# Gain and shift of three normalizations in a transformer block: two fused VectorE passes in place of one VectorE and two GpSimd passes

## The chip, the core and the metric

One NeuronCore of a Trainium2 chip runs the whole kernel. The metric is device time in microseconds, median of several executions. The kernel before ran in 1309.01 us (median of three, 1305.8 to 1310.01).

## What is computed

The input x has 16 batches of 512 nodes with 128 features. Four graph layers follow one another, each fed with relu(layernorm(x)) and added to x. The last layer is a Chebyshev step with a transformer block, and three of its normalizations have a learned gain and shift:

```python
def _layernorm(x, g, b):
    mu = x.mean(-1, keepdims=True)
    var = ((x - mu) ** 2).mean(-1, keepdims=True)
    return (x - mu) / jnp.sqrt(var + EPS_LN) * g + b
...
h = xp @ Wc + bc
h = _layernorm(h, g1, be1)
h = jax.nn.relu(h)
x1 = h + x
...
```

The attention output with x1 as residual goes through the second normalization (g2, be2), then a feed-forward part with gelu (W1, b1, W2, b2), and its result plus residual through the third (g3, be3). g and be are rows of 128 features, the same for every node; mean and variance are one number per node.

## The kernel before

**Layout.** Nodes lie on the 128 partitions in four groups (`NT` = 4), features along the free dimension. A batch of one tensor is thus a tile of 128 x 4 x 128 float32. The rows g1, be1, g2, be2, g3, be3 lie in `rowv`, repeated on every partition; `row[name]` is a 128 x 128 view, `row4(name)` (line 109) the same broadcast over the four groups.

**Stages.** After a front part (constants, the first layer) the function `build_layers` (line 1524) runs a software pipeline over the 16 batches with five stages: gat, edge, cheb, att, ffn (line 1268). In one iteration each stage works on another batch. Every stage is a list of named steps, and each engine executes its own written-out order of them: `FILL_ORDER` for the first iterations, `ORDER` for the loop, `DRAIN_ORDER` for the last ones (lines 1311 to 1519). `run` (line 1643) goes through these lists. Engines execute their steps strictly in that order and meet each other only through semaphores (`ready` and `freed`).

**A normalization** with tag n1, n2 or n3, on y1, y2 or y3, is this sequence: `ln_stats` (four bn_stats, one for each group, VectorE), `ln_aggr` (four bn_aggr giving mean and variance in `mv`, VectorE), `ln_rstd` (GpSimd: add epsilon, then a power of minus one half, into `rs`; lines 1605 and 1607), `ln_apply` (VectorE, line 1632, four tensor_scalar: subtract the mean, times the reciprocal deviation), `affine_g` (GpSimd, line 1637: times the gain row, one instruction over 128 x 512) and `affine_b` (GpSimd, line 1641: plus the shift row). After n1 stands `cheb_x1` (VectorE, line 1911: relu and residual), after n2 `ffn_turn` (TensorE, line 2136: four transposes of y2), after n3 `ffn_final` (VectorE, line 1974).

**The order around n2 and n1 in the loop.** VectorE: `att_scale att_mask2 att_mask3 ffn_y2 n2_stats n2_aggr gat_apply n2_apply att_mask4 cheb_y n1_stats n1_aggr att_mask5 n1_apply gat_scores0 gat_scores1 att_mask6 gat_scores2 att_mask7 gat_scores3 cheb_x1 ... ffn_y3 att_mask8`; and later `n3_stats edge_rden edge_attn edge_u n3_aggr att_mask13 cheb_klow att_mask14 n3_apply att_mask15`. ScalarE: `gat_wh_out0 gat_wh_out1 att_copy2 ffn_x2T att_exp5 att_copy3 ffn_gelu0 ffn_gelu1 att_exp6`. TensorE: `cheb_g gat_turn att_turn2 att_score5 gat_wh ffn_turn att_turn3 gat_s2 ffn_up0 att_score6 ffn_up1 att_turn4 att_score7 ffn_down0 ffn_down1 cheb_x1turn att_turn5 att_score8`. GpSimd: `cheb_rstd edge_rstd ffn_res gat_rstd edge_lo n2_rstd n2_g n2_b n1_rstd n1_g n1_b ffn_b2 gat_low0 ... gat_low3 n3_rstd n3_g n3_b`. `ffn_b2` (line 1740) adds the b2 row to y2 once `ffn_turn` has read it.

**Attention.** For each of 16 tiles TensorE computes a score tile (`att_score`, line 2005), VectorE adds the mask and takes a minimum (`att_mask`, line 1924), ScalarE takes the exponential (`att_exp`, line 1779), TensorE transposes (`att_turn`, line 2106) and ScalarE copies back (`att_copy`, line 1787). `ffn_x2T` is at line 1759, the gelus at line 1769, `ffn_down0` and `ffn_down1` at line 2148. The transposes of `gat_turn` are at line 299, `gat_apply` at line 243.

Of the kernel before, what the change touches and what calls it, by code (L numbers as in the profile page):

```python
# [11 lines left out]
ALU = mybir.AluOpType  # L12
# [5 lines left out]
NT = N // P  # L18
# [325 lines left out]
def build_front(nc, k):  # L344
# [3 lines left out]
    with ExitStack() as c:  # L348
# [938 lines left out]
    "cheb": """  # L1287
        cheb_prop0 cheb_prop1 cheb_g cheb_x1turn cheb_q cheb_k cheb_v cheb_stats cheb_aggr cheb_lo cheb_y
        n1_stats n1_aggr n1_apply cheb_x1 cheb_qlow cheb_klow cheb_apply cheb_hi cheb_xpT cheb_x1T cheb_qsplit
        cheb_ksplit cheb_vout cheb_rstd n1_rstd n1_g n1_b cheb_res stack0 stack2 stack1 stack3 store_v  # L1290
    """.split(),
    "att": """
        att_turn14 att_score0 att_score1 att_turn15 att_rows att_pv0 att_pv1 att_score2 att_turn0 att_score3
# [8 lines left out]
    """.split(),  # L1302
    "ffn": """
        ffn_wo ffn_turn ffn_up0 ffn_up1 ffn_down0 ffn_down1 att_scale ffn_y2 n2_stats n2_aggr n2_apply ffn_y3
        n3_stats n3_aggr n3_apply ffn_final ffn_x2T ffn_gelu0 ffn_gelu1 ffn_res n2_rstd n2_g n2_b ffn_b2 n3_rstd
        n3_g n3_b load_ffn store_out
    """.split(),
}
STAGE_OF = {step: stage for stage, steps in STAGE_STEPS.items() for step in steps}
# [25 lines left out]
        att_exp15 att_copy13 att_copy14 cheb_vout att_copy15  # L1335
    """.split(),
    "POOL": """
        cheb_rstd edge_rstd ffn_res gat_rstd edge_lo n2_rstd n2_g n2_b n1_rstd n1_g n1_b ffn_b2 gat_low0 gat_low1
        gat_low2 gat_low3 n3_rstd n3_g n3_b
    """.split(),  # L1340
    "SP": """
        load_x load_ffn stack1+ stack3+ store_v+ edge_store+ cheb_res load_v stack0 stack2 store_out
# [87 lines left out]
    """.split(),  # L1430
    "POOL": """
        edge_rstd:0 gat_rstd:1 edge_lo:0 gat_low0:1 gat_low1:1 gat_low2:1 gat_low3:1 cheb_rstd:0 edge_rstd:1
        gat_rstd:2 edge_lo:1 n1_rstd:0 n1_g:0 n1_b:0 gat_low0:2 gat_low1:2 gat_low2:2 gat_low3:2 cheb_rstd:1
        edge_rstd:2 gat_rstd:3 edge_lo:2 n1_rstd:1 n1_g:1 n1_b:1 gat_low0:3 gat_low1:3 ffn_res:0 gat_low2:3 gat_low3:3
        cheb_rstd:2 edge_rstd:3 gat_rstd:4 n2_rstd:0 n2_g:0 n2_b:0 edge_lo:3 n1_rstd:2 ffn_b2:0 gat_low0:4 n1_g:2
        n1_b:2 gat_low1:4 gat_low2:4 gat_low3:4 n3_rstd:0 n3_g:0 n3_b:0 cheb_rstd:3 ffn_res:1 edge_rstd:4 gat_rstd:5
        n2_rstd:1 n2_g:1 n2_b:1 edge_lo:4 ffn_b2:1 n1_rstd:3 gat_low0:5 gat_low1:5 n1_g:3 n1_b:3 gat_low2:5 gat_low3:5
        n3_rstd:1 n3_g:1 n3_b:1
    """.split(),
    "SP": """  # L1440
        load_x:1 load_x:2 edge_store:0 cheb_res:0 stack0:0 stack2:0 load_x:3 stack1:0 stack3:0 store_v:0 edge_store:1
# [67 lines left out]
        cheb_rstd:14 ffn_res:12 edge_rstd:15 n2_rstd:12 n2_g:12 n2_b:12 edge_lo:15 n1_rstd:14 n1_g:14 ffn_b2:12
        n1_b:14 n3_rstd:12 n3_g:12 n3_b:12 cheb_rstd:15 ffn_res:13 n2_rstd:13 n2_g:13 n2_b:13 n1_rstd:15 n1_g:15  # L1510
        n1_b:15 ffn_b2:13 n3_rstd:13 n3_g:13 n3_b:13 ffn_res:14 n2_rstd:14 n2_g:14 n2_b:14 ffn_b2:14 n3_rstd:14
        n3_g:14 n3_b:14 ffn_res:15 n2_rstd:15 n2_g:15 n2_b:15 ffn_b2:15 n3_rstd:15 n3_g:15 n3_b:15
# [9 lines left out]


def build_layers(nc, k):
    bank, sem, W, row4 = k.bank, k.kept_sem, k.W, k.row4
    with ExitStack() as c:  # L1526
        def sb(name, shape, dt=F32):
            return c.enter_context(nc.sbuf_tensor(name, shape, dt))
# [21 lines left out]
        h3, y1, x1 = (tile("cheb_" + n) for n in ["hs", "y1", "x1s"])  # L1550
# [11 lines left out]
        xrE, y2, y3, x3E = (tile("ffn_" + n) for n in ["xr", "y2s", "y3s", "x3"])  # L1562
# [81 lines left out]

# [81 lines left out]
        @block.gpsimd  # L1726
        def _(pool):
            def ffn_res(n):
                ready(pool, "ffn_xr", n, 16, 16)
                nc.gpsimd.tensor_tensor(xrE[:], xrE[:], row4("bo"), ALU.add).then_inc(sem("ffn_res"), 1)  # L1730

            def edge_lo(n):
                ready(pool, "edge_hhi", n)
                freed(pool, "edge_gathered", n)
                nc.gpsimd.tensor_tensor(h2_lo[:], h2[:], h2_hi[:].bitcast(F32), ALU.subtract
                                        ).then_inc(sem("edge_hlo"), 1)

# [79 lines left out]
        def _(dve):  # L1817
# [81 lines left out]
                ln_stats(dve, "n1", n, y1)  # L1899

            def n1_aggr(n):
                ln_aggr(dve, "n1", n, ("n1_normed", n, NT))

            def n1_apply(n):
                ln_apply(dve, "n1", n, y1, y1)

            def cheb_x1(n):
                ready(dve, "n1_aff", n, 2, 2)
                freed(dve, "x1_turned", n)
                freed(dve, "res_stored", n, 16)  # L1910
                nc.vector.scalar_tensor_tensor(flat(x1), flat(y1), 0.0, flat(h3), ALU.max, ALU.add
                                               ).then_inc(sem("cheb_x1"), 1)
# [79 lines left out]
        def _(pe):  # L1992
# [198 lines left out]
```

## Time and profile before

| what | value |
|---|---|
| median of three executions | 1309.01 us |
| profiled execution, its own time | 1312.6 us |
| its span | 1310.8 us |
| TensorE matmul busy | 1159.2 us, 88% |
| VectorE busy | 791.7 us, 60% |
| ScalarE busy | 764.0 us, 58% |
| GpSimd busy | 465.6 us, 36% |
| 33 waits of n_rs on n_mv, GpSimd | 181.1 us |

Busy time is the time in which an engine executes a counted instruction, and its share is of the whole span. The front part lasts until about 450 us, the pipeline fills until about 600, repeats a steady period until about 1150, and drains until 1310.8. A wait is the idle time ahead of an instruction, put down to the event that came last. In timelines PE is TensorE, DVE VectorE, ACT ScalarE and POOL GpSimd. Consecutive VectorE instructions overlap a little in the record, so a group's length is a bit more than the distance to the next start.

### The profile page before, as it was taken

Reading aid. Unit: us, or ns where it says so; the run is one execution under the profiler, and the core shown is the slowest. Engines: PE = TensorE matmul, PEld = TensorE weight load, DVE = VectorE, ACT = ScalarE, POOL = GpSimd, SP = SyncE. Lnnn points to the kernel's source line nnn. Section 1 sums busy time; section 2 is a strip of 40 time slices with the busy share of each in tenths; the row PEclk is TensorE's granted clock in tenths of the full one; section 3 lists DMA queues with packets and bytes.
Section 4 is the critical chain, followed back from the end, with each engine's and each line's share of the span. In section 5 each row is a group of like instructions: output and inputs, shape, how many; then the busy total and the mean of one; then the engine's idle time right before and its main releaser. Section 6 shows DMA issues by size and latency. Waiting matters only on the chain. (4 is left out here: it accounts for less than half of the span.)

```text
span 1310.8 us, 24758 instructions
## 1 busy us (share of the span) xinstructions
PE 1159.2 (88%) x7517; PEld 905.1 (69%) x7517; DVE 791.7 (60%) x2832; ACT 764.0 (58%) x1628; POOL 465.6 (36%) x577
## 2 busy tenths in 40 slices
PE   4989999999996957899998999999999999999763
PEld 3658879888884945676776777777777677666542
DVE  6633213212323525688788888888888888877642
ACT  4213324334211313488788788788888878877770
POOL 4203005003123213235445545634634554543423
PEclk7989999999988978699999999999999999999995
DMA  4001020020200000232423423332432342333320
GB/s 118 13 20 42 25 72 1 26 73 1 65 9 1 17 24 17 63 100 74 113 55 93 113 64 88 104 90 64 118 88 64 104 112 56 96 97 94 100 65 17
DMA packets 123748, 83.68 MB, mean 64 GB/s; under 512 B 13216, under 2 KB 106784, under 8 KB 123680
## 3 DMA queue, kind: packets, MB, share of 16 engines
q1 hardware_dynamic: 123680, 82.82, 23.4%
q8 instruction: 37, 0.61, 0.2%
q14 instruction: 31, 0.25, 0.1%
HBM read 28.25 MB, written 20.97 MB: 38 GB/s over the span
## 5 line engine op out<-in xcount | busy, mean ns | idle before, releaser
L1779 ACT ACTIVATE att_Es<-att_Ts,att_small 128x512 f32<-128x512 f32 x256 | 184.9, 722 | 36.0 <-DVE att_small L1924 33.7
L1924 DVE CUSTOM_DVE_ANT_0 att_Ts<-bank,mask_att 128x512 f32<-128x512 f32 x256 | 173.7, 683 | 49.9 <-PE bank L2005 49.3
L2106 PE MATMUL bank<-ident,att_Es 128*128 128x128 f32 x1024 | 156.0, 275 | 22.2 <-ACT att_PTs L1787 21.2
L1787 ACT COPY att_PTs<-bank 128x512 f32<-128x512 f32 x256 | 148.5, 580 | 37.2 <-PE bank L2106 35.2
L2106 PEld LDWEIGHTS bank<-ident,att_Es 128*128 128x128 f32 x1024 | 119.4, 141 | 63.4 <-issue 29.5
L2005 PE MATMUL bank<-K_parts,Q_parts 128*128 128x512 f32 x256 | 123.3, 492 | 0.0
L502 POOL TENSOR_SCALAR l_rs<-l_mv 128x4 f32<-128x4 f32 x16 | 6.9, 432 | 242.5 <-DVE l_mv L712 242.3
L726 DVE TENSOR_TENSOR P_row<-bank,l_bias 128x512 f32<-128x512 f32 x32 | 22.1, 691 | 115.4 <-PE bank L1119 94.1
L1605 POOL TENSOR_SCALAR n_rs<-n_mv 128x4 f32<-128x4 f32 x48 | 12.2, 255 | 182.5 <-DVE n_mv L1600 181.1
L1109 PE MATMUL bank<-G,x0T 128*128 128x128 f32 x384 | 76.0, 280 | 1.1 <-DVE U2T L721 1.0
L1109 PE MATMUL bank<-G,U1T 128*128 128x128 f32 x384 | 75.1, 278 | 0.0
L1109 PE MATMUL bank<-G,U2T 128*128 128x128 f32 x384 | 75.0, 277 | 0.0
L192 POOL TENSOR_SCALAR gat_Vs<-gat_Ts,gat_small 128x512 f32<-128x512 f32 x64 | 50.6, 807 | 67.1 <-DVE gat_small L268 67.0
L1109 PEld LDWEIGHTS bank<-G,x0T 128*128 128x128 f32 x384 | 61.4, 194 | 5.4 <-issue 2.8
L332 PE MATMUL bank<-gat_whs,gat_ETs 128*128 128x128 f32 x512 | 61.9, 275 | 0.0
L332 PEld LDWEIGHTS bank<-gat_whs,gat_ETs 128*128 128x128 f32 x512 | 60.2, 192 | 0.4 <-ACT gat_ETs L218 0.2
L1109 PEld LDWEIGHTS bank<-G,U1T 128*128 128x128 f32 x384 | 59.3, 195 | 0.0
L1109 PEld LDWEIGHTS bank<-G,U2T 128*128 128x128 f32 x384 | 59.1, 194 | 0.0
L2127 PE MATMUL bank<-att_PTs,v_in 128*32 128x512 f32 x512 | 58.5, 597 | 0.0
L2005 PEld LDWEIGHTS bank<-K_parts,Q_parts 128*128 128x128 f32 x256 | 47.4, 190 | 16.1 <-issue 15.7
L1119 PE MATMUL bank<-Z_hi,P3T_hi 128*128 128x512 f32 x128 | 53.0, 414 | 0.0
L212 ACT ACTIVATE gat_Ts<-gat_Vs,gat_small 128x512 f32<-128x512 f32 x64 | 46.4, 730 | 9.4 <-DVE gat_Vs L272 9.4
(301 smaller groups left out, 3028.0 us busy)
## 6 DMA issues: line engine op xcount, KB each, us to landing
Q_parts<-q_hi SPq DMA_DIRECT2D x128, 64.0 KB, 2.0
Q_parts<-q_lo SPq DMA_DIRECT2D x128, 64.0 KB, 2.0
K_parts<-k_hi SPq DMA_DIRECT2D x128, 64.0 KB, 2.0
K_parts<-k_lo SPq DMA_DIRECT2D x128, 64.0 KB, 2.0
l_x<-in_x SPq DMA_DIRECT2D x16, 256.0 KB, 3.0
P2T<-in_x SPq DMA_DIRECT2D x16, 256.0 KB, 4.6
x_after_l<-P2T SPq DMA_DIRECT2D x16, 256.0 KB, 2.3
gat_xin<-x_after_l SPq DMA_DIRECT2D x16, 256.0 KB, 3.1
```

What stands on the lines that cost most here:

```text
L192: nc.gpsimd.tensor_scalar(g.V[:, t, :], g.T[:, t, :], 0.2, small[:, 5, t:t + 1], ALU.mult, ALU.add).then_inc(sem("gat_low"), 1)
L212: nc.scalar.activation(g.T[:, t, :], g.V[:, t, :], ACT.Exp, bias=small[:, 4, t:t + 1], accum_out=small[:, 6, t:t + 1]).then_inc(sem("gat_e ...
L332: mm = nc.tensor.matmul(a0[:, cols(t)], g.ET[:, s, cols(t)], WhA[:, s, 0:D], start=(s == 0), stop=(s == NT - 1))
L726: nc.vector.tensor_tensor(by_batch(zs[:, t, :]), by_batch(bank[t][:]), bias[:, BLOCKS - 1 - lev, t:t + 1, :].broadcast_to([P, CB, D]), ALU.add
L1109: mm = nc.tensor.matmul(bank[t][:, b * D:(b + 1) * D], UT[i][:, b, cols(t)], G[:, STEPS - k0 - i, :], start=(b == 0 and i == 0), stop=(lev ...
L1119: mm = nc.tensor.matmul(bank[t][:], left[:, s, cols(t)], right[:, s, :], start=False, stop=(s == NT - 1 and i == 2))
L1779: nc.scalar.activation(att_E[:, j % RING_E, :], att_T[:, j % RING_T, :], ACT.Exp, scale=-1.0, bias=att_small[:, 0, j:j + 1], accum_out=att ...
L1787: nc.scalar.copy(att_PT[:, i // NT, :, cols(i % NT)], c2[:].rearrange("p (s q) -> p s q", q=P)).then_inc(sem("att_pt"), 1)
L1924: nc.vector.tensor_tensor_reduce(att_T[:, j % RING_T, :], [c0, c1][j % 2][:], k.mask_att[:, j % NT, :], -QK_SCALE, HUGE, ALU.add, ALU.min, ...
L2005: return nc.tensor.matmul(dst, left, right, start=True, stop=True)
L2106: mm = nc.tensor.transpose(c2[:, cols(s)], att_E[:, i % RING_E, cols(s)], k.ident[:])
L2127: mm = nc.tensor.matmul(b0[r, :], vD[:, s, r], att_PT[:, h, s, :], start=(s == 0), stop=(s == NT - 1))
```

## The change

The two GpSimd passes are gone, and so are their steps `n1_g`, `n1_b`, `n2_g`, `n2_b`, `n3_g`, `n3_b` in all three orders. The gain is now applied before the reciprocal deviation: `ln_gain` computes (x - mean) * g in four VectorE instructions, `ln_shift` computes x * rstd + b in four more. `ln_gain` is called at the end of the steps `n1_aggr`, `n2_aggr`, `n3_aggr`, directly behind the aggregates; `ln_shift` replaces `ln_apply` in `n1_apply`, `n2_apply`, `n3_apply`. The two orders of the operations are the same expression. The consumers wait for four `_aff` events in place of two. VectorE's order of steps is unchanged.

```diff
     "POOL": """
-        cheb_rstd edge_rstd ffn_res gat_rstd edge_lo n2_rstd n2_g n2_b n1_rstd n1_g n1_b ffn_b2 gat_low0 gat_low1
-        gat_low2 gat_low3 n3_rstd n3_g n3_b
+        cheb_rstd edge_rstd ffn_res gat_rstd edge_lo n2_rstd n1_rstd ffn_b2 gat_low0 gat_low1
+        gat_low2 gat_low3 n3_rstd 
...
-        def affine_g(pool, tag, n, x, g):
-            ready(pool, tag + "_normed", n, NT, NT)
-            nc.gpsimd.tensor_tensor(x[:], x[:], row4(g), ALU.mult).then_inc(sem(tag + "_aff"), 1)
-
-        def affine_b(pool, tag, n, x, b):
-            ready(pool, tag + "_aff", n, 1, 2)
-            nc.gpsimd.tensor_tensor(x[:], x[:], row4(b), ALU.add).then_inc(sem(tag + "_aff"), 1)
+        def ln_gain(dve, tag, n, x, g):
+            mv = ln_mem[tag][1]
+            ready(dve, tag + "_aggr", n, NT, NT)
+            for t in range(NT):
+                nc.vector.scalar_tensor_tensor(x[:, t, :], x[:, t, :], mv[:, t, 0:1], row[g], ALU.subtract,
+                                               ALU.mult).then_inc(sem(tag + "_gain"), 1)
+
+        def ln_shift(dve, tag, n, x, b):
+            rs = ln_mem[tag][2]
+            ready(dve, tag + "_gain", n, NT, NT)
+            ready(dve, tag + "_rs", n)
+            for t in range(NT):
+                nc.vector.scalar_tensor_tensor(x[:, t, :], x[:, t, :], rs[:, 1, t:t + 1], row[b], ALU.mult,
+                                               ALU.add).then_inc(sem(tag + "_aff"), 1)
...
             def n1_aggr(n):
-                ln_aggr(dve, "n1", n, ("n1_normed", n, NT))
+                ln_aggr(dve, "n1", n, ("n1_aff", n, NT))
+                ln_gain(dve, "n1", n, y1, "g1")
 
             def n1_apply(n):
-                ln_apply(dve, "n1", n, y1, y1)
+                ln_shift(dve, "n1", n, y1, "be1")
 
             def cheb_x1(n):
-                ready(dve, "n1_aff", n, 2, 2)
+                ready(dve, "n1_aff", n, NT, NT)
...
```

n2 and n3 are changed in the same way as n1.

## Rows read from the trace of the kernel before

**Rows 1.** Busy time in one steady period: window, length, us busy (x instructions) by engine, clock, DMA.
```profile
...
899.93:946.90 46.97, 44.54 (x325) 33.91 (x322) 39.76 (x152) 39.59 (x90) 23.52 (x29) 1.00 0.33 89
...
```

**Rows 2.** TensorE's waits from 600 to 1150: us in total, times, longest.
```profile
...
PE bank L2148 <- ACT ffn_mT L1769: 10.3, 12, 0.9
PE bank L1995 <- POOL ffn_y2s L1641: 9.5, 11, 0.9
...
```

**Rows 3.** VectorE's waits, same stretch.
```profile
...
DVE att_Ts L1924 <- PE bank L2005: 25.6, 39, 1.2
DVE cheb_y L1632 <- POOL n_rs L1607: 9.1, 10, 0.9
...
DVE ffn_y2s L1632 <- POOL n_rs L1607: 7.0, 11, 0.7
...
```

**Rows 4.** VectorE, timeline: start us, us, what, idle before and releaser.
```profile
...
933.37 0.38 DVE L1600 BATCH_NORM_AGGREGATE n_mv<-n_stat 128x2 f32<-128x6 f32 x4
...
935.48 1.11 DVE L1632 TENSOR_SCALAR ffn_y2s<-ffn_y2s,n_mv,n_rs 128x128 f32<-128x128 f32 x4 [0.73 <-POOL n_rs L1607]
...
938.85 0.38 DVE L1600 BATCH_NORM_AGGREGATE n_mv<-n_stat 128x2 f32<-128x6 f32 x4
939.20 0.69 DVE L1924 CUSTOM_DVE_ANT_0 att_Ts<-bank,mask_att 128x512 f32<-128x512 f32 x1
...
940.82 1.12 DVE L1632 TENSOR_SCALAR cheb_y<-cheb_y,n_mv,n_rs 128x128 f32<-128x128 f32 x4 [0.92 <-POOL n_rs L1607]
941.85 0.68 DVE L250 CUSTOM_DVE_ANT_0 gat_Ts<-bank,mask_gat 128x512 f32<-128x512 f32 x1
...
945.51 0.90 DVE L1911 SCALAR_TENSOR_TENSOR cheb_x1s<-cheb_y,cheb_hs 128x512 f32<-128x512 f32 x1
...
```

**Rows 5.** TensorE, timeline of the same stretch.
```profile
...
935.96 0.60 PE L299 MATMUL bank<-ident,gat_z 128*128 128x128 f32 x4
...
939.35 0.66 PE L1995 MATMUL bank<-ident,ffn_y2s 128*128 128x128 f32 x4 [0.94 <-POOL ffn_y2s L1641]
...
944.45 2.05 PE L2148 MATMUL bank<-w_W,ffn_mT 128*128 128x128 f32 x16 [0.86 <-ACT ffn_mT L1769]
946.47 0.66 PE L1995 MATMUL bank<-ident,cheb_x1s 128*128 128x128 f32 x4
...
```

**Rows 6.** ScalarE, timeline of the same stretch.
```profile
...
940.54 0.71 ACT L1779 ACTIVATE att_Es<-att_Ts,att_small 128x512 f32<-128x512 f32 x1
...
943.13 1.27 ACT L1769 ACTIVATE ffn_mT<-bank,b1c 128x512 f32<-128x512 f32 x2
...
```

**Rows 7.** GpSimd, timeline of the same stretch.
```profile
...
944.59 1.27 POOL L1740 TENSOR_TENSOR ffn_y2s<-ffn_y2s,rowv 128x512 f32<-128x512 f32 x1
...
```

**Rows 8.** Durations by line, ns min/median/max: old apply, then two fused forms.
```profile
...
L1632 DVE TENSOR_SCALAR ffn_y2s<-ffn_y2s,n_mv,n_rs x64: 337/342/348, 602.2 to 1286.5; 128x128 f32<-128x128 f32 x64
...
L844 DVE SCALAR_TENSOR_TENSOR l_bias<-U2T,pone,l_bias x12: 341/342/344, 57.1 to 60.0; 128x128 f32<-128x128 f32 x12
...
L859 DVE SCALAR_TENSOR_TENSOR G<-Rp,G x36: 279/283/293, 61.6 to 69.5; 128x128 f32<-128x128 f32 x36
...
```

**Rows 9.** VectorE and GpSimd side by side, timeline at 927 and at 1223.
```profile
927.31 0.69 DVE L1889 TENSOR_TENSOR h_lo<-cheb_hs,h_hi 128x512 fp32r<-128x512 f32 x1 [0.85 <-ACT h_hi L1764]
...
926.70 1.04 POOL L1617 TENSOR_TENSOR edge_rs<-edge_rs,neg_half 128x4 f32<-128x4 f32 x1
...
1223.26 1.74 DVE L1911 SCALAR_TENSOR_TENSOR cheb_x1s<-cheb_y,cheb_hs 128x512 f32<-128x512 f32 x1 [1.03 <-POOL cheb_y L1641]
...
1223.18 1.27 POOL L1740 TENSOR_TENSOR ffn_y2s<-ffn_y2s,rowv 128x512 f32<-128x512 f32 x1
...
```

**Rows 10.** VectorE's waits from 1140 to the end.
```profile
...
DVE att_Ts L1924 <- PE bank L2005: 20.4, 24, 2.8
...
```

**Rows 11.** The chain that ended last, its last part: start us, us, what.
```profile
...
1304.67 1.26 POOL ffn_y3s L1637
...
1307.31 0.69 DVE ffn_y3s L1974
...
```

More of the change, by code:

```diff
@@ L1289 @@
         n1_stats n1_aggr n1_apply cheb_x1 cheb_qlow cheb_klow cheb_apply cheb_hi cheb_xpT cheb_x1T cheb_qsplit
-        cheb_ksplit cheb_vout cheb_rstd n1_rstd n1_g n1_b cheb_res stack0 stack2 stack1 stack3 store_v
+        cheb_ksplit cheb_vout cheb_rstd n1_rstd cheb_res stack0 stack2 stack1 stack3 store_v
     """.split(),
@@ L1304 @@
         ffn_wo ffn_turn ffn_up0 ffn_up1 ffn_down0 ffn_down1 att_scale ffn_y2 n2_stats n2_aggr n2_apply ffn_y3
-        n3_stats n3_aggr n3_apply ffn_final ffn_x2T ffn_gelu0 ffn_gelu1 ffn_res n2_rstd n2_g n2_b ffn_b2 n3_rstd
-        n3_g n3_b load_ffn store_out
+        n3_stats n3_aggr n3_apply ffn_final ffn_x2T ffn_gelu0 ffn_gelu1 ffn_res n2_rstd ffn_b2 n3_rstd
+        load_ffn store_out
     """.split(),
@@ L1432 @@
         edge_rstd:0 gat_rstd:1 edge_lo:0 gat_low0:1 gat_low1:1 gat_low2:1 gat_low3:1 cheb_rstd:0 edge_rstd:1
[L1433 to L1438, printed above, removed]
+        gat_rstd:2 edge_lo:1 n1_rstd:0 gat_low0:2 gat_low1:2 gat_low2:2 gat_low3:2 cheb_rstd:1
+        edge_rstd:2 gat_rstd:3 edge_lo:2 n1_rstd:1 gat_low0:3 gat_low1:3 ffn_res:0 gat_low2:3 gat_low3:3
+        cheb_rstd:2 edge_rstd:3 gat_rstd:4 n2_rstd:0 edge_lo:3 n1_rstd:2 ffn_b2:0 gat_low0:4
+        gat_low1:4 gat_low2:4 gat_low3:4 n3_rstd:0 cheb_rstd:3 ffn_res:1 edge_rstd:4 gat_rstd:5
+        n2_rstd:1 edge_lo:4 ffn_b2:1 n1_rstd:3 gat_low0:5 gat_low1:5 gat_low2:5 gat_low3:5
+        n3_rstd:1
     """.split(),
@@ L1508 @@
     "POOL": """
[L1509 to L1512, printed above, removed]
+        cheb_rstd:14 ffn_res:12 edge_rstd:15 n2_rstd:12 edge_lo:15 n1_rstd:14 ffn_b2:12
+        n3_rstd:12 cheb_rstd:15 ffn_res:13 n2_rstd:13 n1_rstd:15
+        ffn_b2:13 n3_rstd:13 ffn_res:14 n2_rstd:14 ffn_b2:14 n3_rstd:14
+        ffn_res:15 n2_rstd:15 ffn_b2:15 n3_rstd:15
     """.split(),
@@ L1524, in build_layers @@
 def build_layers(nc, k):
-    bank, sem, W, row4 = k.bank, k.kept_sem, k.W, k.row4
+    bank, sem, W, row, row4 = k.bank, k.kept_sem, k.W, k.row, k.row4
     with ExitStack() as c:
@@ L1746, in _ @@
                 "n2_rstd": lambda n: ln_rstd(pool, "n2", n), "n3_rstd": lambda n: ln_rstd(pool, "n3", n),
-                "n1_g": lambda n: affine_g(pool, "n1", n, y1, "g1"), "n1_b": lambda n: affine_b(pool, "n1", n, y1, "be1"),
-                "n2_g": lambda n: affine_g(pool, "n2", n, y2, "g2"), "n2_b": lambda n: affine_b(pool, "n2", n, y2, "be2"),
-                "n3_g": lambda n: affine_g(pool, "n3", n, y3, "g3"), "n3_b": lambda n: affine_b(pool, "n3", n, y3, "be3"),
             } | k.gat_steps.POOL(pool))
@@ L1949, in n2_aggr @@
             def n2_aggr(n):
-                ln_aggr(dve, "n2", n, ("n2_normed", n, NT))
+                ln_aggr(dve, "n2", n, ("n2_aff", n, NT))
+                ln_gain(dve, "n2", n, y2, "g2")
             def n2_apply(n):
-                ln_apply(dve, "n2", n, y2, y2)
+                ln_shift(dve, "n2", n, y2, "be2")
             def ffn_y3(n):
@@ L1965, in n3_aggr @@
             def n3_aggr(n):
-                ln_aggr(dve, "n3", n, ("n3_normed", n, NT))
+                ln_aggr(dve, "n3", n, ("n3_aff", n, NT))
+                ln_gain(dve, "n3", n, y3, "g3")
             def n3_apply(n):
-                ln_apply(dve, "n3", n, y3, y3)
+                ln_shift(dve, "n3", n, y3, "be3")
             def ffn_final(n):
-                ready(dve, "n3_aff", n, 2, 2)
+                ready(dve, "n3_aff", n, NT, NT)
                 ready(dve, "ffn_x3", n, 16, 16)
@@ L2136, in ffn_turn @@
             def ffn_turn(n):
-                ready(pe, "n2_aff", n, 2, 2)
+                ready(pe, "n2_aff", n, NT, NT)
                 turn(b0, y2).then_inc(sem("ffn_turned"), 1)
```

## The prediction

> **What bounds the kernel now.** I began with busy time by engine in one period of the steady loop. From one ffn_y3 to the next the period is 46.97 us; TensorE is busy 44.54, VectorE 39.76, ScalarE 39.59, GpSimd 23.52 [rows 1]. GpSimd has the most room, but what counts is which wait stops TensorE. TensorE's two largest waits over twelve periods are short: ffn_down0 on the gelu (12 times, 10.3 us) and ffn_turn on GpSimd's second affine pass (11 times, 9.5 us) [rows 2]. So each period holds 0.86 us of gelu wait and 0.9 us of ffn_turn wait, and between them TensorE runs through. VectorE waits for reciprocal deviations (cheb_y 9.1 us in 10, ffn_y2s 7.0 us in 11), and for scores, 39 times with 25.6 us [rows 3]. The timelines of the stretch 933 to 947 us [rows 4 to 7] show the order in which these meet; everything below is worked out against them. They are one period; the equal waits in rows 2 and 3 say that the others look alike.
>
> **VectorE's added work.** The removed pass is TENSOR_SCALAR, 128x128, median 342 ns [rows 8]; four of them take 1.03 us from the first start to the next instruction's start (940.82 to 941.85) [rows 4]. The new instructions are SCALAR_TENSOR_TENSOR with a scalar from a pointer and two SBUF inputs. Nearest row: L844, the same form at 128x128, 342 ns; with an immediate scalar L859 takes 283 [rows 8]. I take 342, so a group of four costs 1.03 us again; the lower bound is 283, which is 0.24 us less per group. The shift group takes the place of the old apply at no price. The gain group is new: 1.03 us plus about 0.05 for its wait on the aggregates, so 1.08 us, three times per batch, 48 times in all: 52 us of VectorE work. Against it stand 96 GpSimd passes of 1.26 us [rows 11], 121 us; GpSimd is idle half the period anyway [rows 1], so their worth is only in who waited for them.
>
> The Trainium skill, "Vector Engine (DVE) Microarchitecture Reference", section 7 (Points that are easy to get wrong), says that this form with two non-bf16 SBUF sources runs at half throughput. L844 and L859 have two such sources and are as fast as the one-source TENSOR_SCALAR; so the trace speaks against it. I return to it as a rival.
>
> **n2 and ffn_turn.** Before: n2_aggr starts 933.37 and ends 933.75, gat_apply follows, then 0.73 us of wait for GpSimd's power, apply at 935.48 [rows 4]; GpSimd's two passes follow, and ffn_turn starts at 939.35 after 0.94 us of wait [rows 5]. After: gain 933.80 to 934.83, gat_apply to 935.86, shift at once (the power should be ready near 935.5), to 936.89. VectorE is only 0.38 us later, since the gain fills the old wait. gat_apply ends 1.1 us later than before; TensorE's gat_turn is just met (it started at 935.96 [rows 5]). y2 is ready near 937, and TensorE stood free from 938.41 (939.35 less the wait), so ffn_turn starts 0.94 us earlier. That gain holds only if the next meeting point is met too.
>
> **n1 and the gelu: where the gain goes.** Between n2_apply and att_mask5 stands also n1_gain, since the change puts it inside n1_aggr, ahead of att_mask5. Before, n1_aggr started 938.85 and mask5 939.20 [rows 4]; now n1_aggr ends 938.85+0.38+0.38 = 939.61, the gain runs to 940.69, mask5 starts at 940.69 instead of 939.20: 1.49 us later. ScalarE's att_exp5 needs it. It began at 940.54 [rows 6], while mask5 was complete near 939.94 (0.74 us with its accumulator read), so 0.60 us was slack; exp5 comes 0.89 us later. On ScalarE's queue behind exp5 stand att_copy3, a table load and the two gelus [rows 6]; ffn_down0 starts at 944.45+0.89 = 945.34 [rows 5]. TensorE's earlier ffn_turn merely lengthens this wait. So each period grows by 0.89 us, although VectorE keeps idle time elsewhere.
>
> **n1's shift and cheb_x1.** n1_shift can start at 940.69+0.61 = 941.30. The power is ready near 941.20: before, the apply started 1.59 us after n1_aggr's end at 939.23 [rows 4]. On GpSimd ffn_b2 (1.27 us [rows 7]) is now right behind it and starts near 941.27, just ahead of the shift. What two such instructions do to each other shows at 1223 us: cheb_x1 (two SBUF inputs) took 1.74 us beside ffn_b2, against 0.69 elsewhere for its shape [rows 9]: 1.05 us blocked. I take 1.05 (bounds 0 and 1.27). The shift then ends at 943.38 instead of 941.85: 1.53 us late. cheb_x1, no longer beside ffn_b2, gets 0.21 us back (0.90 to 0.69) and ends near 947.73; ffn_down is done at about 947.36, so cheb_x1turn starts 1.28 us later than the 946.47 of before [rows 5]. Without the block it would be 0.89. Downstream, att_score8 and the masks are TensorE-led again and VectorE's lateness dissolves in its waits for scores [rows 3].
>
> **n3.** n3_gain delays mask13 by about 1.1 us, but the masks behind it wait for TensorE's scores, 0.66 us on average [rows 3], several in one stretch. I cost it at nothing; the cover is those waits. If it were gone, up to 1.1 us per period.
>
> **Queues.** No DMA moves. SP's store_out follows ffn_final, which is later only by VectorE's own shift. On GpSimd, ffn_b2, gat_low and the next n_rstd are no longer behind the passes; they wait for VectorE anyway.
>
> **Fill, drain, tail.** In the fill n1's wait for the power, as in the steady part [rows 3], takes the gain in: nothing. In the drain masks wait 20.4 us in 24 cases [rows 10], 0.85 us each, which hides most of a 1.08 us gain; for the n1, n2, n3 groups of batches 13 and 14 I estimate +0.5 each for four, +2 in all (bounds 0 and +4.4). The tail of batch 15 is a pure chain: the two GpSimd passes of n3 stand in it from 1304.67 to 1307.31 [rows 11], 2.64 us, and those of n2 for as long; both pairs disappear; the gains hide behind the power. That is -5.3 us (bounds -3 and -5.3, if the gains hold up the power's start).
>
> **Sum.** 12 x 1.28 = +15.4, +2, -5.3: +12.1 us on the profiled execution's own 1312.6, which is 3.6 above the median of the runs. Applied to the median, 1309.0 + 12 = 1321. Without the block 12 x 0.89 gives +7.4: 1316.
>
> **Rivals.**
> (a) *GpSimd's passes were the price, and the gelu is not late.* If exp5 were on time, TensorE would keep the 0.9 us of ffn_turn: 11 x -0.9 = -10, with the tail -5.3: 1294. For it: GpSimd heads the second largest wait. The place is mask5's start; it decides at 0.60 us of lateness, and I get 1.49. With gains at 283 ns (three groups before exp5, -0.7) I get 0.8, still late. Chance 0.08.
> (b) *Partly absorbed.* No block, and an instruction at or near 283 ns: 0.2 to 0.6 us per period, +2.4 to +7.2, drain 0 to +2, tail -5.3: 1306 to 1313. Chance 0.12.
> (c) *Gains are blocked by the power.* n_rstd's power (1.04 us) now runs beside each gain. If it held VectorE for its whole length, mask5 would be about 2 us later: 12 x 2 = +24, 1345. Against it: h_lo, two SBUF inputs, started at 927.31 within the power of 926.70 and took its usual 0.69 [rows 9]. A milder form, 0.5 to 1 us per period from hand-overs with the short GpSimd instructions, gives 1327 to 1333. Chance of both 0.16, mostly the milder.
> The Trainium skill, "SBUF — State Buffer", section "Who interferes with whom", has one exclusive lock held for a whole instruction between such a VectorE instruction and a GpSimd one that reads SBUF. By it the case at 1223 us is expected and the one at 927 us is not: there the trace disagrees.
> (d) *Half throughput.* From 283 at 128 to 690 at 512 columns a column costs 1.06 ns; half speed adds 0.14 us per instruction, 12 before mask5: +1.6 us per period, 1341. Chance 0.04.
>
> **Numbers.** The main case, with or without the block, has 0.60: 1315 to 1325, point 1321. A measurement here tells about 0.3% (4 us) from no change. Faster: (a) and little of (b), 0.10. Same: most of (b), 0.12. Slower 0.78. The range reaches from (b) to the milder (c): 1309 to 1335.
>
> **What would show it.** Period near 48.2 us; ffn_turn's wait gone; ffn_down0's wait on the gelu up from 0.86 to near 2.7; exp5 waiting for mask5 0.9 us or more; n1_shift's first instruction at about 1.4 us or its group at 2.1; SCALAR_TENSOR_TENSOR median 342; the tail 5 us shorter. A gelu wait that stays under 1 us with a period under 47 would prove me wrong.

## The result, and the profile after

The changed kernel took 1339.31 us (median of four executions, 1331.78 to 1347.21) beside 1309.51 for the kernel before in the same series: ratio 1.0227, interval 1.0176 to 1.0277. A second series gave the same ratio (1341.53, 1.0192 to 1.0263). It is slower, as forecast, but by 30 us, and the forecast was 12 with a range that ended at 1335. The profiled execution is the slowest of its series: 1347.21, span 1345.4, 34.6 over the span before. The second series has a profile of its own with a span of 1335.7.

The head of the page after: busy time by engine, and three rows of the 40 slices.

```profile
PE 1171.4 (87%) x7517; PEld 912.9 (68%) x7517; DVE 851.1 (63%) x3024; ACT 761.9 (57%) x1628; POOL 346.8 (26%) x481
...
PE   4989999999978957798899898899899899889764
...
PEclk8989999999998968999999999999999999999986
```

VectorE rose by 59 us (791.7 before), GpSimd fell by 119 (465.6), as the instruction counts say. TensorE is busy 12 us longer (1159.2) with the same 7517 matmuls; 8.5 us of this lie in the six periods whose clock reads under 1.00 (one of them is in the windows below), and 4.7 in the two after them. It is the first number that the forecast has no place for.

Every batch has one `ffn_y3`; its sixteen starts cut the span into parts. Three of the windows between them, in the order window, length, busy us of PE, PEld, DVE, ACT and POOL (x instructions), granted clock, DMA share, GB/s:

```profile
669.82:721.84 52.02, 47.02 (x321) 36.03 (x322) 42.98 (x164) 38.45 (x86) 13.07 (x19) 0.93 0.30 82
...
920.41:969.35 48.94, 44.71 (x324) 33.77 (x323) 43.46 (x164) 39.34 (x89) 16.12 (x23) 1.00 0.32 86
...
1260.37:1303.83 43.46, 32.40 (x209) 21.61 (x208) 23.49 (x76) 31.84 (x68) 5.41 (x6) 0.88 0.34 90
```

The middle one answers to [rows 1]: 48.94 us for 46.97, with TensorE as busy as before, so about 1.8 us more of waiting. The first has a clock of 0.93, TensorE busy 2.3 us longer than there, and 52.02 us. The kernel before has 1.00 in every one of its first 14 windows.

The terms of the forecast against both profiles of the changed kernel, each as difference to the profile before, in us:

| part | forecast | after | after, second profile |
|---|---|---|---|
| up to the first ffn_y3 | 0 | +3.1 | +3.4 |
| the next 12 periods | +15.4 | +28.0 | +21.3 |
| the two after that (drain) | +2 | +7.1 | +4.1 |
| last period and end (tail) | -5.3 | -3.6 | -3.8 |
| sum | +12.1 | +34.6 | +24.9 |

TensorE's waits from 600 to 1150 after (us in total, times, longest), to hold against [rows 2]:

```profile
PE bank L2158 <- ACT ffn_mT L1776: 14.9, 11, 1.6
PE bank L2011 <- DVE att_oTs L1946: 14.0, 11, 2.0
PE bank L2116 <- ACT att_PTs L1794: 8.9, 18, 0.7
...
PE bank L2005 <- DVE cheb_x1s L1919: 2.6, 8, 0.3
```

The wait of `ffn_turn` for GpSimd is gone, as forecast. The gelu's grew from 0.86 to 1.35 in the mean and 1.6 at most; I had 2.7 there, and part of that is met earlier, in the third row, before the transposes that follow `ffn_turn`. The second row, `ffn_wo` waiting for `att_oTs`, has no term in the forecast; it was 7.6 us before. VectorE's own waits, same stretch, tell what is late there:

```profile
DVE att_Ts L1932 <- PE bank L2015: 22.3, 36, 3.3
DVE gat_stat L231 <- DMA gat_xin<-x_after_l: 14.3, 11, 1.9
```

The waits for reciprocal deviations of [rows 3] are gone, filled by the gains. VectorE now waits 1.3 us per period for a load, `gat_xin`, and `att_oTs` stands behind it. Both rows stood in the same views of the kernel before, at about half the size:

```profile
PE bank L2001 <- DVE att_oTs L1938: 7.6, 11, 1.8
DVE gat_stat L231 <- DMA gat_xin<-x_after_l: 7.8, 11, 1.8
```

The prediction passed over them: it wrote that TensorE "runs through" between its two largest waits. They were the sign that the path over `gat_xin` had no slack.

### The profile page after: what moved, and what is told of

Same layout as the page of the kernel before. It is cut to its first block and busy times, and to the rows that moved or that the text cites. A ratio compares the mean times of both kernels' runs of the same rounds, so it can differ in the third digit from the quotient of the medians.

```text
span 1345.4 us, 24882 instructions
## 1 busy us (share of the span) xinstructions
PE 1171.4 (87%) x7517; PEld 912.9 (68%) x7517; DVE 851.1 (63%) x3024; ACT 761.9 (57%) x1628; POOL 346.8 (26%) x481
## 5 line engine op out<-in xcount | busy, mean ns | idle before, releaser
L2116 PE MATMUL bank<-ident,att_Es 128*128 128x128 f32 x1024 | 159.8, 280 | 33.0 <-ACT att_PTs L1794 32.6
L1605 POOL TENSOR_SCALAR n_rs<-n_mv 128x4 f32<-128x4 f32 x48 | 15.0, 313 | 260.7 <-DVE n_mv L1600 260.6
L2015 PEld LDWEIGHTS bank<-K_parts,Q_parts 128*128 128x128 f32 x256 | 48.4, 194 | 17.5 <-issue 15.7
L2158 PE MATMUL bank<-w_W,ffn_mT 128*128 128x128 f32 x256 | 37.4, 305 | 20.4 <-ACT ffn_mT L1776 20.4
L2158 PEld LDWEIGHTS bank<-w_W,ffn_mT 128*128 128x128 f32 x256 | 34.2, 213 | 28.1 <-ACT ffn_mT L1776 27.9
```

The costliest lines, as they stand in the source:

```text
L1605: nc.gpsimd.tensor_scalar(rs[:, 0, :], mv[:, :, 1], EPS, None, ALU.add).then_inc(sem(tag + "_vareps"), 1)
L2015: return nc.tensor.matmul(dst, left, right, start=True, stop=True)
L2116: mm = nc.tensor.transpose(c2[:, cols(s)], att_E[:, i % RING_E, cols(s)], k.ident[:])
L2158: mm = nc.tensor.matmul(b0[:, cols(t)], mT[:, q, cols(t)], k.W2[:, q, :], start=(q == 0), stop=(q == 1))
```

## The path around n2 and n1

VectorE in one period, to compare with [rows 4]; columns are start, us, instruction and, in brackets, idle time before it:

```profile
954.96 1.14 DVE L1639 SCALAR_TENSOR_TENSOR ffn_y2s<-ffn_y2s,n_mv,rowv 128x128 f32<-128x128 f32 x4
...
957.04 1.13 DVE L1647 SCALAR_TENSOR_TENSOR ffn_y2s<-ffn_y2s,n_rs,rowv 128x128 f32<-128x128 f32 x4
...
960.85 1.14 DVE L1639 SCALAR_TENSOR_TENSOR cheb_y<-cheb_y,n_mv,rowv 128x128 f32<-128x128 f32 x4
961.90 0.69 DVE L1932 CUSTOM_DVE_ANT_0 att_Ts<-bank,mask_att 128x512 f32<-128x512 f32 x1
...
962.52 2.07 DVE L1647 SCALAR_TENSOR_TENSOR cheb_y<-cheb_y,n_rs,rowv 128x128 f32<-128x128 f32 x4
...
968.18 0.68 DVE L1919 SCALAR_TENSOR_TENSOR cheb_x1s<-cheb_y,cheb_hs 128x512 f32<-128x512 f32 x1
```

A gain group takes 1.14 us and a shift group 1.13. The shift of n1 takes 2.07, because of this row of GpSimd's timeline, which in [rows 7] started 3.8 us after the old apply of [rows 4] and now starts 0.14 before the shift:

```profile
962.38 1.27 POOL L1747 TENSOR_TENSOR ffn_y2s<-ffn_y2s,rowv 128x512 f32<-128x512 f32 x1
```

ScalarE and TensorE, to compare with [rows 6] and [rows 5]:

```profile
962.63 0.72 ACT L1786 ACTIVATE att_Es<-att_Ts,att_small 128x512 f32<-128x512 f32 x1 [1.48 <-DVE att_small L1932]
...
965.23 1.27 ACT L1776 ACTIVATE ffn_mT<-bank,b1c 128x512 f32<-128x512 f32 x2
```

```profile
959.52 0.60 PE L2005 MATMUL bank<-ident,ffn_y2s 128*128 128x128 f32 x4
960.80 0.63 PE L2116 MATMUL bank<-ident,att_Es 128*128 128x128 f32 x4 [0.68 <-ACT att_PTs L1794]
...
966.55 2.05 PE L2158 MATMUL bank<-w_W,ffn_mT 128*128 128x128 f32 x16 [1.63 <-ACT ffn_mT L1776]
968.91 0.66 PE L2005 MATMUL bank<-ident,cheb_x1s 128*128 128x128 f32 x4 [0.31 <-DVE cheb_x1s L1919]
```

`att_exp5` waits 1.48 us for mask 5, the gelus follow, `ffn_down0` waits 1.63. From `ffn_wo` to `ffn_down0` it was 14.11 us (930.34 to 944.45 before) and is 15.11 (951.44 to 966.55): +1.0, where I had 0.89. `cheb_x1turn` waits another 0.31 and starts 2.36 us behind `ffn_down0` for 2.02. Both together explain 1.34 of the 1.97 us (from one `cheb_x1turn` to the next it is 46.97 and 48.94). The remaining 0.63 lies between `cheb_x1turn` and `ffn_wo`: 899.50 to 930.34 before, 919.97 to 951.44 after.

## The path that the forecast missed

VectorE's timeline after, behind `ffn_y3` of 920.41:

```profile
934.68 1.14 DVE L1639 SCALAR_TENSOR_TENSOR ffn_y3s<-ffn_y3s,n_mv,rowv 128x128 f32<-128x128 f32 x4
...
936.34 0.68 DVE L1926 TENSOR_TENSOR k_lo<-bank,k_hi 128x512 fp32r<-128x512 f32 x1
...
949.41 0.87 DVE L231 BATCH_NORM_STATS2 gat_stat<-gat_xin 128x6 f32<-128x128 f32 x4 [1.14 <-DMA gat_xin<-x_after_l]
```

SyncE's queue in the same stretch, first after, then before (the time is that of issuing):

```profile
937.19 0.51 SPq L1701 DMA_DIRECT2D K_parts<-k_hi  x1
937.74 0.59 SPq L1701 DMA_DIRECT2D K_parts<-k_lo  x1
...
945.04 0.45 SPq L1714 DMA_DIRECT2D out_x<-ffn_y3s  x1
946.25 0.39 SPq L177 DMA_DIRECT2D gat_xin<-x_after_l  x1
```

```profile
916.10 0.51 SPq L1694 DMA_DIRECT2D K_parts<-k_hi  x1
...
925.17 0.39 SPq L177 DMA_DIRECT2D gat_xin<-x_after_l  x1
```

n3's gain stands ahead of `att_mask13` and `cheb_klow`. `cheb_klow` makes `k_lo`, and the copies of K wait for it: they are issued 0.17 us after it ends. Twelve K and Q copies, the output store and the load of `gat_xin` then leave SyncE's queue one after the other. From the first K copy to the load is 9.07 us before and 9.06 after. The queue's only wait for an operand in this stretch is the one for `k_lo`; issuing the twelve copies and the store takes 7.4 of the 9 us, and the gaps between them are the same in both kernels. The first copy is 16.17 us behind `ffn_y3` before (899.93) and 16.78 after, 0.61 late, and those 0.61 arrive whole, 9 us later, at `gat_xin`; `gat_stats` waits 1.14 us for it (0.30 before), `att_oT` is behind it on VectorE, and TensorE's `ffn_wo` is behind that. Here it is before, then after:

```profile
930.34 0.94 PE L2001 MATMUL bank<-w_Wo,att_oTs 128*128 128x128 f32 x6 [0.40 <-DVE att_oTs L1938]
951.44 0.82 PE L2011 MATMUL bank<-w_Wo,att_oTs 128*128 128x128 f32 x5 [1.24 <-DVE att_oTs L1946]
```

That is the 0.63. No DMA was moved by the change, and one became late all the same.

## The experiments

My theory: the loop's cost is the sum of three waits, each with a place: the gelu (n1's gain ahead of mask 5), the blocked shift (`ffn_b2` beside n1's shift), and SyncE's chain (n3's gain ahead of `cheb_klow`). Rivals: the fused instructions themselves cost it, wherever they stand; or the lowered clock does, by itself. The table has the difference to the profile before by part, as above, the mean of eight loop periods (fourth to twelfth ffn_y3), and the recorded ratio of the runs with its 95% interval, which can differ from the quotient of the two medians by up to 0.2%.

| kernel | to first ffn_y3 | 12 periods | drain | tail | loop period | median | ratio |
|---|---|---|---|---|---|---|---|
| before | | | | | 47.04 | 1309.5 | |
| after | +3.1 | +28.0 | +7.1 | -3.6 | 49.23 | 1339.31 | 1.0227 (1.0176 to 1.0277) |
| after again | +3.4 | +21.3 | +4.1 | -3.8 | 48.96 | 1341.53 | 1.0227 (1.0192 to 1.0263) |
| n1 gain late | +2.3 | +20.1 | +3.3 | -2.3 | 48.89 | 1331.59 | 1.0175 (1.0150 to 1.0199) |
| ffn_b2 after shift | -1.4 | +24.4 | +3.6 | -3.7 | 49.22 | 1343.71 | 1.0260 (1.0237 to 1.0283) |
| n3 gain late | +2.6 | +13.2 | +6.5 | -3.4 | 48.18 | 1332.06 | 1.0169 (1.0145 to 1.0193) |
| all three | +0.3 | +4.7 | +5.7 | -5.1 | 47.14 | 1320.06 | 1.0088 (1.0058 to 1.0117) |
| n1 alone | -1.7 | +6.0 | +2.6 | -0.8 | 47.57 | 1320.77 | 1.0097 (1.0077 to 1.0117) |
| n2 alone | -0.3 | +2.6 | +4.4 | -1.1 | 47.21 | 1315.23 | 1.0051 (1.0031 to 1.0071) |
| n3 alone | -1.8 | +5.9 | -0.1 | -1.0 | 47.74 | 1315.73 | 1.0061 (1.0041 to 1.0081) |
| batch 15 alone | -1.8 | -0.7 | +2.2 | -3.6 | 46.92 | 1303.34 | 0.9954 (0.9937 to 0.9972) |
| all three, drain old | -1.6 | +5.2 | +1.0 | -3.8 | 47.23 | 1313.20 | 1.0012 (0.9992 to 1.0031) |
| the same, fill old too | -1.7 | +4.1 | +1.6 | -4.1 | 47.13 | 1308.83 | 0.9979 (0.9957 to 1.0001) |

A part's difference comes from one execution of each kernel, the medians from 4 to 23. The first column reaches to the first `ffn_y3` and so holds a part of the fill: the first gain group of the changed kernel starts at 521.1 us. Three versions with the old form in all of that part (n3 alone, batch 15 alone, the last) have -1.7 to -1.8, so the one profile before is itself 1.8 us off there, and a single part is good to about 2 us.

**n1's gain behind mask 5.**

```diff
             def n1_aggr(n):
                 ln_aggr(dve, "n1", n, ("n1_aff", n, NT))
-                ln_gain(dve, "n1", n, y1, "g1")
...
             def n1_apply(n):
+                ln_gain(dve, "n1", n, y1, "g1")
                 ln_shift(dve, "n1", n, y1, "be1")
```

> The changed kernel, with n1's gain moved from the end of n1_aggr into n1_apply, so that att_mask5 no longer stands behind it; nothing else moves and no work is taken away. Theory A (the gelu chain behind att_mask5 and the late cheb_x1 are two parallel paths to cheb_x1turn): the gelu wait of ffn_down0 falls from 1.6 us to under 0.9 per period, but cheb_x1 is as late as before, so its wait grows from 0.3 to about 1 us and the period stays within 0.3 us of the changed kernel's 48.8: total 0 to -4 us against the changed kernel, about 1335. Rival B (the gelu chain alone sets the loss): the period falls by 0.9 us or more, total about 1327. Rival C (VectorE is simply short of time, placement does not matter): gelu wait and period both unchanged.

Measured: 1331.59 us. The gelu is nearly on time again, and the period at full clock is still 48.9. TensorE's timeline of one period (912.80 to 961.69) has the time in another place:

```profile
957.77 2.05 PE L2158 MATMUL bank<-w_W,ffn_mT 128*128 128x128 f32 x16 [0.96 <-ACT ffn_mT L1776]
961.26 0.66 PE L2005 MATMUL bank<-ident,cheb_x1s 128*128 128x128 f32 x4 [1.43 <-DVE cheb_x1s L1919]
```

The gain now delays n1's shift, which still meets `ffn_b2` (2.03 us), and `cheb_x1turn` takes over what `ffn_down0` gave back. The mechanism at the gelu is shown (its wait falls from 1.63 to 0.96); that removing it alone would free the period is refuted. The median is 7.7 us below the changed kernel's, where at most 4 was expected. Its profile has one of the 12 periods below a clock of 1.00, the changed kernel's two profiles have six and two; whether that is the difference is not shown.

**`ffn_b2` behind n1's shift.** GpSimd's wait alone was added.

```diff
                 ready(pool, "ffn_turned", n)
+                need(pool, sem("n1_aff"), {0: 3, 1: 3, 12: 15}.get(n, B) * NT if isinstance(n, int) else (n + 3) * NT)
```

> The changed kernel, with one wait more on GpSimd: ffn_b2 waits until n1's shift is done. Theory A: the shift group of n1 falls from 2.1 to 1.1 us, cheb_x1 is no longer waited for, and the period falls only by the 0.3 us that TensorE waited for cheb_x1: total -3 to -5 us against the changed kernel, about 1335. Rival (the shift is slow by itself, from the second SBUF input or the pointer, not from GpSimd's instruction): the group stays at 2.1 us. Rival C (VectorE short of time): taking 1 us of VectorE time away gives the full 1 us per period, total -12 or more.

Measured: 1343.71 us, no gain where 3 to 5 us were expected. The shift group fell from 2.07 to 1.14 us, so the block is `ffn_b2` and is worth 0.93. `cheb_x1turn` no longer waits; loop periods at full clock are 48.4 to 48.9, at most 0.4 shorter: in the period at 48.42 `ffn_down0` still waits 1.63 us for the gelu. Its loop mean is no better: seven of its 12 periods have a clock of 0.97 to 0.99, and some of these took 50 us.

**n3's gain behind `cheb_klow` and mask 14.** The same edit as the first, for n3.

> The changed kernel, with n3's gain moved from the end of n3_aggr into n3_apply, behind att_mask13, cheb_klow and att_mask14. Theory A (k_lo comes 0.9 us late, and behind it stand on SP's queue the transfers of K's parts, store_out and then the load of gat_xin, whose lateness reaches gat_stats, att_scale and TensorE's ffn_wo): the K parts, the gat_xin load and ffn_wo come about 0.9 us earlier relative to cheb_x1turn, VectorE's wait for gat_xin falls from 1.14 to about 0.3 us, TensorE's wait for att_oT from 1.2 to 0.5; period 48.8 to about 48.0, total -8 to -12 us against the changed kernel, about 1329. Rival C (VectorE short of time): no change of period. Rival (the gat_xin wait comes from slower DMA): the load's issue moves but the wait stays.

Measured: 1332.06 us, 7.3 below the changed kernel where 8 to 12 were expected, and loop periods at full clock 48.0: 0.85 less than after, as expected. `ffn_wo`'s waits for `att_oTs` fell from 9.8 to 2.2 us over eight loop periods. Measured from `ffn_y3`, the load of `gat_xin` is issued 25.02 us later (25.84 after, 25.24 before). This is the missed term, removed with one moved line.

**All three together.**

> The changed kernel with all three: n1's gain and n3's gain late, and ffn_b2 behind n1's shift. VectorE does the same work as in the changed kernel. Theory A: the two parallel paths to cheb_x1turn shorten together, by about 1.1 us, and the SP chain by 0.9: period near 47.0, as before the change, with the tail 2 to 5 us shorter: total 1300 to 1312. Rival C (VectorE short of time): the period stays over 48.3, total over 1327.

Measured: 1320.06 us, loop period 47.14. The total is above the expected 1300 to 1312; the period is as expected, 0.1 above before, with all 48 gain groups still on VectorE: 42.59 us busy in a period of 47.14 where it had 39.76. So 1.8 of the 1.9 us per period (48.96 in the second profile of the changed kernel) are places, not work, and the first rival falls. The windows' row of a period:

```profile
904.87:952.01 47.14, 44.52 (x324) 33.85 (x323) 42.59 (x165) 39.40 (x89) 15.98 (x23) 1.00 0.33 89
```

What is left of the cost (1320.06 against 1310.53) has left the loop. It is in the drain (+5.7) and in the first three of the 12 periods (+3.8 of the +4.7). In the drain, windows of 5 us show this:

```profile
1240.00:1245.00 5.00, 2.23 (x14) 1.44 (x14) 3.60 (x12) 3.64 (x9) 0.00 (x0) 1.00 0.37 91
1245.00:1250.00 5.00, 4.88 (x50) 3.22 (x54) 1.44 (x5) 2.24 (x5) 0.00 (x0) 0.66 0.68 189
...
1260.00:1265.00 5.00, 4.05 (x15) 3.13 (x16) 1.75 (x6) 3.19 (x8) 0.00 (x0) 0.50 0.41 124
```

TensorE is busy 2.23 us of the first 5, after waits for the attention's copies (1.58 us the longest here). In the next window its clock is 0.66, and later 0.50, the lower of its two levels (1.2 GHz): four transposes at 1246.52 take 1.08 us where 0.60 is usual. Whether the waits brought the clock down is not shown. The version below with the new form in batch 15 alone has the old code in all of this stretch (its first new instruction starts at 1285), and its profile has a drain part of +2.2 us and these windows:

```profile
1245.00:1250.00 5.00, 2.47 (x15) 1.78 (x15) 3.72 (x17) 3.33 (x9) 1.60 (x3) 1.00 0.42 105
1250.00:1255.00 5.00, 3.69 (x17) 2.92 (x17) 2.10 (x6) 3.36 (x8) 2.24 (x3) 0.63 0.51 147
```

The profile before has a window as little busy (2.48 us from 1250 to 1255), and the clock stays at 1.00 behind it.

**One normalization alone.** Each of these has the new form for one tag and the old form, GpSimd's passes included, for the other two.

```diff
             def n3_aggr(n):
-                ln_aggr(dve, "n3", n, ("n3_normed", n, NT))
+                ln_aggr(dve, "n3", n, ("n3_aff", n, NT))
+                ln_gain(dve, "n3", n, y3, "g3")
```

> The kernel before, with the new form for n1 alone (its gain directly behind the aggregates). Theory A (meeting points): the shift of n1 is blocked by ffn_b2 for about 1 us, cheb_x1 comes near 0.9 us later, the gelu wait grows by about 0.5; period 47.0 to about 47.9, total +8 to +12 us, near 1321. Rival C (each group of VectorE work costs alike, wherever it stands): the three parts cost the same, +0.6 us per period each, total +7 to +10 us for each of n1, n2, n3.

> The kernel before, with the new form for n2 alone. Theory A: VectorE is only 0.4 us later at att_mask5, within its slack of 0.6 us; ffn_turn's wait of 0.9 us goes, but cheb_x1, now 0.4 us later and still behind n1's two GpSimd passes, keeps the period: 47.0 to 47.4. The tail is 2.7 us shorter. Total -4 to +3 us, near 1310. Rival (GpSimd's passes on n2 were the price, so their removal is a gain of 0.9 us per period): total -12 us or more. Rival C: +7 to +10 us.

> The kernel before, with the new form for n3 alone. Theory A: k_lo comes 0.9 us later, then the K parts, store_out and the load of gat_xin on SP's queue; VectorE's wait for gat_xin and TensorE's for att_oT grow by 0.7 to 0.9 us: period 47.0 to about 47.8; tail 2.7 us shorter; total +5 to +9 us, near 1318. Rival (n3 is hidden, as forecast): period 47.0, total -3 us.

Measured, against 1308.75 for the kernel before in this series: n1 +12.0, n2 +6.5, n3 +7.0 us, and in the loop +0.5, +0.2 and +0.7 per period. n1 and n3 are within what was expected; n2 is not (-4 to +3): its loop period is (47.21), but its drain part is +4.4 and its tail gave back 1.1 where 2.7 was expected. The sum of the three loops, 1.4, is below the 1.9 of the whole: n1 beside n2 costs more than alone, probably since n2's own delay on VectorE then stands before mask 5 too; that was not tried apart. n2 alone shows why the 0.9 us of `ffn_turn` bought nothing. Its waits of TensorE over eight loop periods:

```profile
PE bank L2163 <- ACT ffn_mT L1783: 8.4, 8, 1.1
PE bank L2121 <- ACT att_PTs L1801: 5.4, 8, 0.7
PE bank L2010 <- DVE cheb_x1s L1925: 3.9, 8, 0.5
```

The 7.3 us of waiting for GpSimd in those eight periods before are gone; the transposes behind wait 5.4 for ScalarE's copies, the gelu 1.5 more, `cheb_x1` 3.9. TensorE only reached the next late operand sooner. n3 alone has SyncE's chain without the other two: its waits in eight loop periods are

```profile
PE bank L2016 <- DVE att_oTs L1952: 9.4, 8, 1.3
PE bank L2010 <- POOL ffn_y2s L1656: 7.5, 8, 1.0
PE bank L2163 <- ACT ffn_mT L1783: 6.9, 8, 0.9
```

with the lower two unchanged against before (7.3 and 6.9) and the first up from 4.0 to 9.4: 0.68 us per period, all of the 0.70 by which its period grew. Its first K copy is issued 17.00 us after `ffn_y3`, against 16.17 before.

**The last batch alone.** The kernel before, with the new form only for n2 and n3 of batch 15, where nothing else is left to run.

> The kernel before in all but the last batch: the new form for n2 and n3 of batch 15 alone, where no other work stands beside them. Theory A: the pure chain of the tail loses twice the two GpSimd passes, 2.64 us each, and gains nothing: -4 to -5.3 us, near 1305.5, faster than both kernels. Rival (the gains hold up the start of the power through the shared port, as L1614 took 0.51 instead of 0.23 us beside ffn_final): -3 to -4.

Measured: 1303.34 us, ratio 0.9954 (0.9937 to 0.9972), in medians 5.4 us faster than the kernel before, and the only version whose interval lies below 1. Its chain of waits ends so, to compare with [rows 11]:

```profile
1300.64 0.39 POOL n_rs L1605
...
1302.25 0.15 DVE ffn_y3s L1647
...
1302.51 0.88 DVE ffn_y3s L1647 x3
...
1303.42 0.69 DVE ffn_y3s L1999
```

From the last `ffn_y3` to the end it takes 8.43 us for 10.88: two passes of GpSimd (2.64) less 0.15 by which the gain holds up the deviation's first instruction (0.39 for 0.24).

**Where the rest of the cost sits.** From the version with all three repairs, the old form was put back in the drain, then in the fill as well, so that the last has the new form in the steady loop and in batch 15's n2 and n3. Where the old form came back, the added wait of `ffn_b2` went too.

> The version with all three repairs (n1's and n3's gains beside their shifts, ffn_b2 behind the aff copies), with the old single pass and GpSimd's two passes put back in the drain of the pipeline only: n1 of batches 14 and 15, n2 and n3 of batches 12 to 14. Batch 15's n2 and n3 keep the new form. That version took 1320.06 us, 9.5 to 11.5 over before. Theory: what is left of its cost sits in the drain (last periods 44.25 and 44.84 us against 42.72 and 40.69 before, with the granted clock down to 0.50 to 0.66 in single stretches) and in the fill (51.66 against 48.61). Then this gives 1313 to 1316, the drain's periods are back within 0.5 us of before, and the granted clock stays at 1.00 there. Rival, the leftover is spread over the loop by the clock, which dips wherever TensorE has waited a little longer: then this stays at 1318 to 1321 and its periods of the loop are over 47.3 on average.

> As the last, with the old form in the fill too (n1 of batches 0 to 3, n2 and n3 of batches 0 and 1), so that the new form stands only in the steady loop and in batch 15's end. Theory, the loop itself costs nothing once the three waits are repaired (its periods read 47.0 to 47.3 against 46.9 to 47.0) and the end of batch 15 gives back 4 to 6 us: 1303 to 1308, near the version that is new in batch 15 alone (1303.34). Rival, the loop pays too: over 1311.

> The changed kernel as it is, again, since its four runs spread over 15 us (1331.78 to 1347.21) with mean granted clocks of 0.952 to 0.968, where the kernel before spreads over 8. Theory, the change costs about 1.9 us in every period of the loop at full clock (48.8 against 46.95) and the rest is periods in which the clock was lowered: 1333 to 1342, and in its trace the periods at a clock of 1.00 are 48.6 to 48.9 and all longer ones go with a clock under 1.00. Rival, the longer periods are a property of their place in the program and not of the clock: then the same periods are long again, at a clock of 1.00 too.

Measured: 1313.20, 1308.83 and 1341.53 us. The drain was worth 7 us of the 9.5 (its part fell from +5.7 to +1.0), in the range of the expectation; the two intervals of the ratio are apart. The fill is not settled: 1308.83 lies just above the expected 1303 to 1308, the medians differ by 4 us, but the intervals overlap and the parts differ by 1 us, and the last profile still has two periods of 50 us with a clock of 0.97. Putting the new form into the loop thus gains nothing over batch 15 alone (0.9979 with an interval that reaches 1.0001, against 0.9954); at 47.13 for 47.04 us per period the loop itself costs next to nothing. For the changed kernel, seven loop periods in a row stand at a clock of 1.00 with 48.70 to 49.02 us. Two of these had 49.90 and 49.74 at 0.99 and 0.97 in the first profile, and the second period of all had 52.02 at 0.93 and now has 48.49 at 1.00. So these go with the clock and not with their place. Two others were long and below 1.00 in both profiles (the third, 50.03 and 50.98; the eleventh, 50.10 and 49.87); for them place and clock are not told apart. At a clock of 1.00 the loop still costs 1.9 us more per period than before, so the lowered clock by itself does not explain it.

## Why the prediction was wrong in size

- **Cost of the instructions: right.** The new form takes 340 to 347 ns in median, and 342 was taken. The half throughput of rival (d) is not there.
- **n2 and ffn_turn: right.** The wait of 0.94 is gone, and the time went into the next operand, as n2 alone shows.
- **n1 and the gelu: right in place and size.** +1.0 for 0.89 between `ffn_wo` and `ffn_down0`, though less of it shows as the gelu's wait than I wrote.
- **n1's shift and `ffn_b2`: right.** Group 2.07 for 2.08 forecast, block 0.93 for 1.05, undone by one added wait.
- **n3: the step that failed.** I wrote that n3's gain "delays mask13 by about 1.1 us, but the masks behind it wait for TensorE's scores ... I cost it at nothing". The masks did have that cover. `cheb_klow`, which stands between mask 13 and mask 14 in the very order that I quoted, had none: what waits for it is a queue that issues one DMA behind the other for 9 us. The step's own upper bound, 1.1 us per period, was right, and neither the point nor the range used it. In the changed kernel it cost 0.63 per period, alone 0.70, and moving n3's gain gave back 0.85. The row that would have said so is TensorE's third wait, for `att_oTs`, which the prediction did not read. "No DMA moves" under Queues was true and answered the wrong question, which was whether one becomes late.
- **The range.** 12 times 0.63 us is 7.6 and would have put the sum near 1329, inside the range. The rest of the profiled differences lies in the periods with a lowered clock, the fill, the drain and the tail. The 12 periods gave +21 where two of them were below a clock of 1.00 (second profile) and +28 where six were (first profile), against 15.4 + 7.6 = 23. The forecast had no term for a lowered clock; the profile before shows none in the pipeline from 613.6 to 1265.6 us.
- **Fill and drain: too small.** Fill was put at 0; up to the first `ffn_y3` it is +3.1 and +3.4 against the one profile before, and 1.8 more against the three versions with the old form there. Which wait costs it was not looked for. The drain was put at +2 and gave +4.1 and +7.1; the bounds, 0 to +4.4, came from masks that had cover and had no term for the clock, which reads 0.96 and 0.88 in the two periods of the first profile and 1.00 and 0.92 in the second. A single drain part can be 2 us off, as batch 15 alone shows.
- **Tail: right in sign, -3.6 to -3.8 for -5.3** in the single profiles; after the last `ffn_y3` 1.9 of n3's 2.64 came back, and 1.7 to 1.9 of as much before it. In medians batch 15 alone gave 5.4.
- **Rivals.** (a) is refuted by n2 alone: with GpSimd's passes gone there, nothing came back. (b) fell with the period: 1.9 us more, and its bound was 0.6. (c), gains blocked by the power, did not happen (below).

What lowered the clock and what it costs by itself, apart from the waits before it, stays open: no run here changed the clock alone.

## What to carry to other kernels

When an instruction is put ahead of others on an engine, price it by every consumer of what stands behind it, and ask of each whether the consumer has slack; a queue that issues back to back had none here, and handed a delay on to its last transfer. A cover that holds for most of the instructions behind (here the masks) says nothing about the one that differs. A short wait that stands in every period, as the one for `att_oTs` did, says that the path behind it has little slack. In this kernel trading GpSimd's work for VectorE's paid only where the work was a pure chain, in the last batch; elsewhere the best placement only brought it back to even.

## What was not expected of the hardware

- A power on GpSimd beside a group of fused VectorE instructions with two SBUF inputs held up neither by much: the gains of n1 have 343, 347 and 355 ns as minimum, median and maximum over the 48 between 600 and 1170 us, and of the powers the longest took 1.17 us for 1.04. GpSimd's 128x512 addition beside the same form made one instruction take up to 1292 ns instead of 340. The Trainium skill, "SBUF — State Buffer", section "Who interferes with whom", has a shared port pair with an exclusive lock, for which a VectorE instruction with two SBUF inputs contends with a GpSimd instruction that reads SBUF. The second number agrees with it. By the first, the power cannot have held that lock for all of its 1.04 us.
- In the other direction the effect is small: GpSimd's 128x4 addition took 0.39 us beside a gain in the tail and 0.24 without. It took 0.38 once in the kernel before too, at 933.95 beside `gat_apply`.
- In a kernel whose TensorE is about 90% busy, the clock of single periods read 0.93 to 0.99, in part at other places in another execution; in the drain it read 0.66 and 0.50 over 5 us behind a window with 2.23 us busy, and 1.00 behind one with 2.48 in another execution.
